# Attention stage: every unit's column sums on TensorE, none of the second pair additions on GpSimd or VectorE

## The chip, the cores and the metric

The kernel runs on one core of a Trainium2 chip. The metric is the device time of one execution in microseconds (us); less is better. The chip's engines run their own instruction streams and meet at semaphores: TensorE (PE, with its weight loads PEld), VectorE (DVE), ScalarE (ACT), GpSimd (POOL), and SyncE (SP), which issues the DMAs.

## What is computed

Eight images of 384 channels and 32 x 32 pixels go through three stages, one after the other on the chip: a convolution with a local correlation, an attention with 12 heads of width 32 over the 1024 pixels, and a feed-forward layer. The change touches the attention alone, of which this is the core (t is the image as 1024 tokens of 384 channels):

```python
q = (x @ Wq.T).reshape(b, n, H, HD).transpose(0, 2, 1, 3)     # H = 12, HD = 32
...
scores = jnp.einsum('bhqd,bhkd->bhqk', q, k) * SCALE
probs = jax.nn.softmax(scores, axis=-1)
out = jnp.einsum('bhqk,bhkd->bhqd', probs, v)
...
t = t + _L1_attn_ref(_ln_t(t), ...)
```

The softmax needs, for each query, the maximum over the keys, the exponentials and their sum. The kernel divides by the sum only after the weighing with v.

## The kernel before, in words

**Units.** The attention works on one image in 24 units (IU): three groups of four heads, eight units in a group. A unit u covers for the four heads two key tiles of 128 (256 keys) and one half of the queries (512 of 1024). So four units (u%4 = 0 to 3) make one block: all keys for one half of the queries, and six blocks x make an image. Scores stand transposed, keys on the partitions and queries along the free axis.

**What a unit does.** TensorE makes 8 score matmuls (`scores`, L892, 4 steps s of 2) into three PSUM banks `st`; ScalarE turns each into exponentials in SBUF (`exponentials`, L1259, tiles `ex`, two sets of four, one per parity of u). TensorE weighs v with the exponentials of the unit before (`weigh(u-1, 0)` and `weigh(u-1, 1)`, L926): each call is four 32-column matmuls of 512 columns in float32, side by side in the array by `tile_position`, and float32 makes two instructions of each, so 8 instructions. They add into the bank `pv`.

**Maxima.** Beside that, 8 matmuls per unit (`max_scores`, L905) make scores of the next group of heads, queries on the partitions, into two banks `mx`, turn by turn; VectorE takes the maximum of each (`take_max`, L1067), which frees its bank. The matmul of item n waits until the reduction of item n-2 is done. Every second unit VectorE folds 16 partial maxima (`combine`, L1073), TensorE transposes them (`turn`, L911), ScalarE copies the row (L1248) and a DMA writes it beside the queries.

**Column sums.** The sum over keys of the exponentials is taken in steps. GpSimd adds the two key tiles of a unit per head (L1416, `pair`, 8 tiles: four per parity). In an odd unit it then adds the pair of the even unit before it (L1420), so that one tile stands for two units. TensorE multiplies it with ones (`sum_up`, L940, again 8 instructions) into the bank `sm`: one such call in every even unit, for the two units before it, and one in the epilogue. In the last eight units of the last image there are no maxima to take, and VectorE makes the second addition (L1145) in GpSimd's place.

**Division.** When a block's sums are complete, VectorE takes their reciprocals in four quarters (`invert_sum`, L1082) and multiplies (`attended`, L1087); ScalarE and GpSimd split the result in high and low halves (L1273, L1352) for the output projection.

**Other work in the units.** In units 6 to 23 the projections of the next image's q, k and v (`project_part`, L854, L864: 5 and 4 matmuls of 512 columns, or 36 of 128), in units 0 to 5 the output projection of the image before (`out_project`, L877). The normalisation of the next image's tokens lies in units 0 to 6, 21 and 23: additions on GpSimd (`fold`, L1366, L1369; also `add`, L1361, in units 0 to 5), VectorE's `centre`, `invert_std`, `normalise`, `z_low` (L1030, L1036, L1042, L1048), and two square roots on ScalarE, each with a change of its function table.

**What sets the order.** Each engine's list is written out by hand in its own `unit(b, u, ...)`; engines are in order. VectorE's list is: `combine` in even units, then for n = 0 to 7 `beside(n)`, which holds the extra work placed at that point, and then the reduction of item n. TensorE's order in a unit is scores 0, projection (5), maximum 0, projection (4), [turn], scores 1, maximum 1, weigh 0, maxima 2 and 3, scores 2, weigh 1, maximum 4, [var or mean], scores 3, maximum 5, [sum_up in even units], maxima 6 and 7. (`maximum(s, e)` is item 2s+e.) A loop covers images 0 to 5; it turns round between units 5 and 6.

Of the kernel before, what the change touches and what calls it, by code (L numbers as in the profile page):

```python
# [17 lines left out]
ALU = mybir.AluOpType  # L18
# [538 lines left out]
def attention_stage(nc, x_in, w_q, w_k, w_v, w_o, b_o, identity, out, n_images):  # L557
# [17 lines left out]
    HG = P // HEAD  # L575
# [16 lines left out]
    with ctx:  # L592
# [74 lines left out]
        pair_added = N.sem("pair_added")  # L667
# [144 lines left out]
        def _(pe):  # L812
# [120 lines left out]
            def sum_up(b, u):  # L933

                w = u % UNITS
                pe.wait_ge(pair_added, STEPS // 2 * (IU * b + u + 1))
                if w % 4 == 1:
                    wait(pe, sum_inverted, 4 * (6 * b + u // 4))
                for h in range(HG):
                    last = nc.tensor.matmul(sm[h * HEAD:(h + 1) * HEAD, :], ones[:, :],  # L940
                                            pair[HG + h][:, :], start=w % 4 == 1,
                                            stop=w % 4 == 3, tile_position=(0, h * HEAD))
                last.then_inc(sum_ready, 1)
# [21 lines left out]
            def unit(b, u, out_proj=True, norm=True, qkv=True, maxima=True, load=False):  # L965
# [3 lines left out]
                lag = (b, u - 1) if u else (b - 1, IU - 1)  # L969
                lagging = not (isinstance(b, int) and b == 0 and u == 0)  # L970
                if u == FIRST and qkv:


                    free[id(pj)] = (std_ready, 2 * b + 4)
# [19 lines left out]
                maximum(0, 1)  # L994
                if lagging:
                    weigh(*lag, 0)
                maximum(1, 0)

                maximum(1, 1)
                scores(b, u, 2)  # L1000
                if lagging:
                    weigh(*lag, 1)
# [8 lines left out]
                if lagging and u % 2 == 0:  # L1011
                    sum_up(*lag)
# [3 lines left out]
            def epilogue(b):  # L1016
                weigh(b, IU - 1, 0)
                weigh(b, IU - 1, 1)
                sum_up(b, IU - 1)
# [6 lines left out]
        def _(dve):  # L1026
# [49 lines left out]
            def invert_sum(b, x, quarter):  # L1076

                at = slice(quarter * QUARTER, (quarter + 1) * QUARTER)
                dve.wait_ge(sum_ready, 2 * (6 * b + x + 1))
# [54 lines left out]
            def unit(b, u, out_proj=True, norm=True, qkv=True, maxima=True, load=False):  # L1134
# [4 lines left out]
                def maximum(s, e):  # L1139
                    if maxima:  # L1140
                        take_max(group, 8 * w + 2 * s + e)
                    elif u % 2 and e == 1:
                        dve.wait_ge(pair_ready, STEPS * (IU * b + u) + s + 1)
                        both = pair[HG + s]
                        nc.vector.tensor_tensor(both[:, :], both[:, :], pair[s][:, :], ALU.add  # L1145
                                                ).then_inc(pair_added, 1)

                def beside(n):

                    if not maxima:  # L1150
                        if u % 4 == 1 and n == 0:
                            for quarter in range(4):
                                invert_sum(b, (u - 5) // 4, quarter)
                            attended(b, (u - 5) // 4)
                        return
                    if started and u % 4 == 1 and n in (0, 1, 7):
                        invert_sum(b, (u - 5) // 4, min(n, 2))
                    if started and u % 4 == 2 and n == 0:
                        invert_sum(b, (u - 6) // 4, 3)
                        attended(b, (u - 6) // 4)  # L1160
# [185 lines left out]
        def _(pool):  # L1346
# [49 lines left out]
            def unit(b, u, out_proj=True, norm=True, maxima=True, load=False, **_flags):  # L1396
                unit_no = IU * b + u
                started = not (isinstance(b, int) and b == 0 and u < 4)
                for s in range(STEPS):
# [9 lines left out]
                    if u % 2 and s == 0:  # L1409

                        wait(pool, sum_ready, IU // 2 * b + u // 2)
                    if u % 2 == 0 and not (isinstance(b, int) and b == 0 and u == 0):

                        pool.wait_ge(pair_added, STEPS // 2 * (unit_no - 2) + s + 1)
# [3 lines left out]
                    if u % 2 and maxima:  # L1418
                        pool.wait_ge(pair_ready, STEPS * unit_no + s + 1)
                        nc.gpsimd.tensor_tensor(both[:, :], both[:, :], pair[s][:, :], ALU.add  # L1420
                                                ).then_inc(pair_added, 1)
# [387 lines left out]
```

## Time and profile before

| what | us |
|---|---|
| median of 3 runs | 3200.16 |
| lowest and highest of the runs | 3199.73, 3200.5 |
| span of the profiled execution, first to last instruction | 3196.4 |
| attention units, first score matmul to the end of the stage | 529.6 to 2371.9 |
| mean granted TensorE clock over the span | 0.948 |

The profiled execution has no time of its own beside its span; the runs are 3.8 us above the span, which is what lies around the instructions. The profile names an engine's instructions by line, with the tiles written and read, and gives for each group the busy time, the mean of one, and the idle time of the engine before it with the one that ended it. The times of a timeline are counted from the first instruction. The duration of a matmul holds the way through the array; the distance from the start of one to the start of the next is what it costs in a stream.

### The profile page before, as it was taken

The numbers are of one execution on the slowest core, as the hardware profiler recorded it, in microseconds if no ns is written. First come the engines' busy times: TensorE is split into PE (matmuls) and PEld (weight loads), VectorE is DVE, ScalarE is ACT, GpSimd is POOL, SyncE is SP. The second block draws the span as 40 slices with busy tenths as digits, with TensorE's granted clock in tenths as the row PEclk, the third lists the DMA queues.
The fourth block names the chain that finished last, engine by engine and source line by source line (L and its number), as shares of the span: only waits on it lengthen the run. The fifth ranks groups of instructions, "written<-read, shape, count | busy, mean of one in ns | idle before, by whom it ended". The sixth has DMA issues, their size and how long they took to land. (4 is left out here: it accounts for less than half of the span.)

```text
span 3196.4 us, 52214 instructions
## 1 busy us (share of the span) xinstructions
PE 2839.4 (89%) x16784; PEld 1108.5 (35%) x16784; DVE 2046.0 (64%) x2855; ACT 1550.0 (48%) x2582; POOL 1851.1 (58%) x1407
## 2 busy tenths in 40 slices
PE   4988668898899898898898898999858999999999
PEld 3544222233233233333332332332113444444444
DVE  6777247878778778778778778777634334334332
ACT  2333023556556556556556556555534444444443
POOL 2222023899899899799899899989951110110110
PEclk9888777999999999999999999999978999999999
DMA  3233222011111111111211211112020011010110
GB/s 140 79 114 104 95 77 66 21 54 27 61 54 28 61 54 28 65 51 28 71 44 28 76 39 34 60 27 67 1 99 20 20 40 35 24 39 20 39 39 20
DMA packets 68759, 163.91 MB, mean 51 GB/s; under 512 B 13585, under 2 KB 17614, under 8 KB 67470
## 3 DMA queue, kind: packets, MB, share of 16 engines
q1 hardware_dynamic: 68494, 160.67, 15.7%
q8 instruction: 131, 2.15, 0.3%
q14 instruction: 134, 1.10, 0.1%
HBM read 59.20 MB, written 37.75 MB: 30 GB/s over the span
## 5 line engine op out<-in xcount | busy, mean ns | idle before, releaser
L1067 DVE TENSOR_REDUCE b_mxp<-b_mx 128x1 f32<-128x512 f32 x1536 | 1002.4, 680 | 375.3 <-PE b_mx L905 368.2
L1416 POOL TENSOR_TENSOR b_pair<-b_ex 128x512 f32<-128x512 f32 x768 | 1001.5, 1313 | 162.9 <-ACT b_ex L1259 152.5
L1259 ACT ACTIVATE b_ex<-b_st 128x512 f32<-128x512 f32 x1536 | 829.2, 595 | 544.1 <-PE b_st L892 540.0
L905 PE MATMUL b_mx<-b_kst,b_qst 96*128 96x512 f16 x1536 | 568.1, 394 | 109.6 <-DVE b_mxp L1067 92.0
L892 PE MATMUL b_st<-b_qst,b_kst 97*128 97x512 f16 x1536 | 472.2, 386 | 32.0 <-issue 17.8
L1420 POOL TENSOR_TENSOR b_pair<-b_pair 128x512 f32<-128x512 f32 x368 | 476.5, 1295 | 28.9
L1630 DVE TENSOR_TENSOR c_gs<-c_g,c_gs 128x512 f16<-128x512 f32 x192 | 132.6, 691 | 466.2 <-ACT c_gs L1703 466.2
L1555 PE MATMUL c_hid<-c_z,c_wi 128*128 128x512 f16 x1728 | 406.8, 381 | 16.4 <-DVE c_z L1623 16.4
L926 PE MATMUL b_pv<-b_ex,b_v 128*32 128x512 f32 x3072 | 412.9, 610 | 1.0 <-ACT b_ex L1259 1.0
L1570 PE MATMUL c_acc<-c_gs,c_wo 128*128 128x512 f16 x1728 | 403.9, 379 | 0.0
L905 PEld LDWEIGHTS b_mx<-b_kst,b_qst 96*128 96x128 f16 x1536 | 132.9, 97 | 716.5 <-DVE b_mxp L1067 597.3
L1736 POOL TENSOR_TENSOR c_xs<-c_x 128x512 f32<-128x512 f32 x16 | 21.1, 1319 | 484.2 <-DMA c_x<-after_attention 481.9
L1699 ACT ACTIVATE c_g<-c_hid,c_bias 128x512 f32<-128x512 f32 x192 | 131.4, 685 | 345.6 <-PE c_hid L1555 345.4
L1555 PEld LDWEIGHTS c_hid<-c_z,c_wi 128*128 128x128 f16 x1728 | 168.4, 98 | 237.5 <-issue 29.6
L1570 PEld LDWEIGHTS c_acc<-c_gs,c_wo 128*128 128x128 f16 x1728 | 169.1, 98 | 203.9
L892 PEld LDWEIGHTS b_st<-b_qst,b_kst 97*128 97x128 f16 x1536 | 149.6, 99 | 190.8 <-ACT b_ex L1259 46.1
L1082 DVE RECIPROCAL b_inv<-b_sm 128x128 f32<-128x128 f32 x192 | 180.4, 944 | 9.3 <-PE b_sm L940 9.3
L506 POOL TENSOR_TENSOR a_sqs<-a_sq 128x1024 f32<-128x1024 f32 x8 | 18.8, 2354 | 218.1 <-ACT a_sq L484 218.1
L854 PE MATMUL b_pj<-b_z,b_wq 128*128 128x512 f16 x405 | 117.2, 420 | 20.6 <-issue 10.8
L1703 ACT ACTIVATE c_gs<-c_g 128x512 f16<-128x512 f32 x192 | 120.9, 629 | 6.1
L1736 POOL TENSOR_TENSOR c_xs<-c_sq 128x512 f32<-128x512 f32 x16 | 20.3, 1266 | 174.0 <-ACT c_sq L1680 174.0
L877 PE MATMUL b_pj<-b_ao,b_wo 128*128 128x512 f16 x432 | 112.3, 409 | 8.5 <-ACT b_ot L1280 6.6
(153 smaller groups left out, 2928.6 us busy)
## 6 DMA issues: line engine op xcount, KB each, us to landing
a_x<-in_x SPq DMA_DIRECT2D x8, 1536.0 KB, 7.1
a_ob<-a_x SPq DMA_DIRECT2D x8, 1536.0 KB, 7.1
after_conv<-a_ob SPq DMA_DIRECT2D x24, 512.0 KB, 2.6
b_xl<-after_conv SPq DMA_DIRECT2D x8, 1536.0 KB, 6.4
b_qst<-b_staged0q SPq DMA_DIRECT2D x192, 64.0 KB, 2.0
b_kst<-b_staged0k SPq DMA_DIRECT2D x192, 64.0 KB, 2.0
b_v<-b_vstaged SPq DMA_DIRECT2D x24, 512.0 KB, 3.0
b_xr<-after_conv SPq DMA_DIRECT2D x8, 1536.0 KB, 6.4
```

What stands on the lines that cost most here:

```text
L892: nc.tensor.matmul(st[(SCORES * u + n) % NST][:, :], kst[g][0:MAXROW + 1, s, kt * P:(kt + 1) * P], qst[g][0:MAXROW + 1, s, half * BANK:(ha ...
L905: nc.tensor.matmul(mx[item % 2][:, :], qst[g][0:MAXROW, h, t * P:(t + 1) * P], kst[g][0:MAXROW, h, half * BANK:(half + 1) * BANK], start=T ...
L926: last = nc.tensor.matmul(pv[h * HEAD:(h + 1) * HEAD, :], v[g][:, kt, h * HEAD:(h + 1) * HEAD], ex[u % 2 * HG + h][:, e * BANK:(e + 1) * B ...
L1067: nc.vector.reduce_max(mxp[h % 2][:, t, half:half + 1], mx[item % 2][:, :], AX_X).then_inc(mx_taken, 1)
L1082: nc.vector.reciprocal(inv[:, at], sm[:, at]).then_inc(sum_inverted, 1)
L1259: nc.scalar.activation(ex[u % 2 * HG + s][:, e * BANK:(e + 1) * BANK], st[(SCORES * u + n) % NST][:, :], ACT.Exp, scale=SCALE).then_inc(ex ...
L1416: nc.gpsimd.tensor_tensor(both[:, :], e[:, 0:BANK], e[:, BANK:NPIX], ALU.add).then_inc(pair_ready, 1)
L1420: nc.gpsimd.tensor_tensor(both[:, :], both[:, :], pair[s][:, :], ALU.add).then_inc(pair_added, 1)
L1555: last = nc.tensor.matmul(hid[m % NH][:, :], wi[a][:, k, m * P:(m + 1) * P], z[p][b][:, k, :], start=n == 0, stop=n == 8)
L1570: last = nc.tensor.matmul(acc[j][:, :], wo[a][:, m, j * P:(j + 1) * P], gs[m % NS][b][:, :], start=m == 0 and n == 0, stop=m == MC - 1 and ...
L1630: nc.vector.tensor_tensor(gs[m % NS][1][:, :], g[m % NG][:, :], gs[m % NS][0][:, :], ALU.subtract).then_inc(glo_ready, 1)
L1699: nc.scalar.activation(g[m % NG][:, :], hid[m % NH][:, :], ACT.Gelu, bias=bias[:, m:m + 1], scale=1.0 / WSCALE).then_inc(gelu_ready, 1)
```

## The change

The second additions (L1420 on GpSimd, L1145 on VectorE) and their semaphore go. `sum_up` is called for every unit, two units late, and takes that unit's own pair tiles. It stands directly before the two calls of `weigh`, which now follow each other, so that TensorE makes 24 float32 instructions in one run. Items 2 and 3 of the maxima and scores 2 are moved around that run. GpSimd waits before the first pair of a unit for the sum of two units before. VectorE's four reciprocals of a block, which stood at n = 0, 1, 7 of the unit u%4 = 1 and n = 0 of the next, all stand at n = 4 to 7 of the unit u%4 = 1.

```diff
--- before.py
+++ after.py
@@ -664,7 +664,6 @@
         st_ready = N.sem("st_ready")
         exp_ready = N.sem("exp_ready")
         pair_ready = N.sem("pair_ready")
-        pair_added = N.sem("pair_added")
         pv_ready = N.sem("pv_ready")
         sum_ready = N.sem("sum_ready")
         pv_moved = N.sem("pv_moved")
@@ -933,12 +932,12 @@
             def sum_up(b, u):
 
                 w = u % UNITS
-                pe.wait_ge(pair_added, STEPS // 2 * (IU * b + u + 1))
-                if w % 4 == 1:
+                pe.wait_ge(pair_ready, STEPS * (IU * b + u + 1))
+                if w % 4 == 0:
                     wait(pe, sum_inverted, 4 * (6 * b + u // 4))
                 for h in range(HG):
                     last = nc.tensor.matmul(sm[h * HEAD:(h + 1) * HEAD, :], ones[:, :],
-                                            pair[HG + h][:, :], start=w % 4 == 1,
+                                            pair[u % 2 * HG + h][:, :], start=w % 4 == 0,
                                             stop=w % 4 == 3, tile_position=(0, h * HEAD))
                 last.then_inc(sum_ready, 1)
 
@@ -967,7 +966,9 @@
                 group = GROUPS * b + g + 1
                 image = b + 1 if g == GROUPS - 1 else b
                 lag = (b, u - 1) if u else (b - 1, IU - 1)
+                before = (b, u - 2) if u > 1 else (b - 1, IU + u - 2)
                 lagging = not (isinstance(b, int) and b == 0 and u == 0)
+                summing = not (isinstance(b, int) and b == 0 and u < 2)
                 if u == FIRST and qkv:
 
 
@@ -992,14 +993,14 @@
 
                 scores(b, u, 1)
                 maximum(0, 1)
+                maximum(1, 0)
+                if summing:
+                    sum_up(*before)
                 if lagging:
                     weigh(*lag, 0)
-                maximum(1, 0)
-
+                    weigh(*lag, 1)
+                scores(b, u, 2)
                 maximum(1, 1)
-                scores(b, u, 2)
-                if lagging:
-                    weigh(*lag, 1)
                 maximum(2, 0)
                 if norm and u in (1, 2):
                     var(b + 1, u - 1)
@@ -1008,14 +1009,13 @@
 
                 scores(b, u, 3)
                 maximum(2, 1)
-                if lagging and u % 2 == 0:
-                    sum_up(*lag)
                 maximum(3, 0)
                 maximum(3, 1)
 
             def epilogue(b):
                 weigh(b, IU - 1, 0)
                 weigh(b, IU - 1, 1)
+                sum_up(b, IU - 2)
                 sum_up(b, IU - 1)
                 for i in range(6):
                     out_project(b, i)
@@ -1076,7 +1076,7 @@
             def invert_sum(b, x, quarter):
 
                 at = slice(quarter * QUARTER, (quarter + 1) * QUARTER)
-                dve.wait_ge(sum_ready, 2 * (6 * b + x + 1))
+                dve.wait_ge(sum_ready, 4 * (6 * b + x + 1))
                 if quarter == 0:
                     wait(dve, att_ready, 6 * b + x)
                 nc.vector.reciprocal(inv[:, at], sm[:, at]).then_inc(sum_inverted, 1)
@@ -1139,25 +1139,15 @@
                 def maximum(s, e):
                     if maxima:
                         take_max(group, 8 * w + 2 * s + e)
-                    elif u % 2 and e == 1:
-                        dve.wait_ge(pair_ready, STEPS * (IU * b + u) + s + 1)
-                        both = pair[HG + s]
-                        nc.vector.tensor_tensor(both[:, :], both[:, :], pair[s][:, :], ALU.add
-                                                ).then_inc(pair_added, 1)
 
                 def beside(n):
 
+                    if started and u % 4 == 1 and n in (4, 5, 6, 7):
+                        invert_sum(b, (u - 5) // 4, n - 4)
+                    if started and u % 4 == 2 and n == 0:
+                        attended(b, (u - 6) // 4)
                     if not maxima:
-                        if u % 4 == 1 and n == 0:
-                            for quarter in range(4):
-                                invert_sum(b, (u - 5) // 4, quarter)
-                            attended(b, (u - 5) // 4)
                         return
-                    if started and u % 4 == 1 and n in (0, 1, 7):
-                        invert_sum(b, (u - 5) // 4, min(n, 2))
-                    if started and u % 4 == 2 and n == 0:
-                        invert_sum(b, (u - 6) // 4, 3)
-                        attended(b, (u - 6) // 4)
                     if n == 3 and u >= FIRST and qkv:
                         stage_low(b + 1, u - FIRST)
                     if load and u in (21, 23) and n in (5, 6):
@@ -1406,19 +1396,11 @@
                     if u < FIRST and out_proj and s == 2:
                         add(b - 1, u)
                     pool.wait_ge(exp_ready, SCORES * unit_no + 2 * s + 2)
-                    if u % 2 and s == 0:
-
-                        wait(pool, sum_ready, IU // 2 * b + u // 2)
-                    if u % 2 == 0 and not (isinstance(b, int) and b == 0 and u == 0):
-
-                        pool.wait_ge(pair_added, STEPS // 2 * (unit_no - 2) + s + 1)
+                    if s == 0 and not (isinstance(b, int) and b == 0 and u < 2):
+                        pool.wait_ge(sum_ready, unit_no - 1)
                     e, both = ex[u % 2 * HG + s], pair[u % 2 * HG + s]
                     nc.gpsimd.tensor_tensor(both[:, :], e[:, 0:BANK], e[:, BANK:NPIX], ALU.add
                                             ).then_inc(pair_ready, 1)
-                    if u % 2 and maxima:
-                        pool.wait_ge(pair_ready, STEPS * unit_no + s + 1)
-                        nc.gpsimd.tensor_tensor(both[:, :], both[:, :], pair[s][:, :], ALU.add
-                                                ).then_inc(pair_added, 1)
 
             def epilogue(b):
                 attended_low(b, 5)
```

## Rows read from the trace of the kernel before

**Rows 1.** Head of the profile's page.
```profile
span 3196.4 us, 52214 instructions
```
**Rows 2.** Busy time by stretch: all units; fourth image, units 0-6 and 7-23.
```profile
core 0: us, PE busy (x) PEld busy (x) DVE busy (x) ACT busy (x) POOL busy (x), PEclk, DMA share, GB/s
529.61:2371.86 1842.25, 1671.32 (x9694) 555.13 (x9692) 1411.94 (x2084) 1068.58 (x1969) 1645.92 (x1284) 0.97 0.14 43
1222.62:1306.20 83.58, 68.21 (x328) 20.92 (x328) 66.33 (x94) 48.83 (x81) 70.54 (x55) 0.92 0.20 65
1306.20:1459.05 152.85, 146.59 (x937) 53.00 (x935) 116.70 (x180) 87.56 (x169) 138.74 (x111) 1.00 0.14 39
```
**Rows 3.** Groups of instructions by line (busy us, mean ns, idle before, by whom ended).
```profile
L1259 ACT ACTIVATE b_ex<-b_st 128x512 f32<-128x512 f32 x1536 | 829.2, 595 | 544.1 <-PE b_st L892 540.0 <-POOL b_pair L1416 2.8
L1420 POOL TENSOR_TENSOR b_pair<-b_pair 128x512 f32<-128x512 f32 x368 | 476.5, 1295 | 28.9
```
**Rows 4.** TensorE's timeline, unit 9 of the fourth image (start us, length us, ...).
```profile
1324.18 1.24 PE L854 MATMUL b_pj<-b_z,b_wk 128*128 128x512 f16 x5
1325.26 0.38 PE L905 MATMUL b_mx<-b_kst,b_qst 96*128 96x512 f16 x1
...
1326.78 0.38 PE L905 MATMUL b_mx<-b_kst,b_qst 96*128 96x512 f16 x1
1327.09 1.06 PE L926 MATMUL b_pv<-b_ex,b_v 128*32 128x512 f32 x8
1328.09 0.60 PE L905 MATMUL b_mx<-b_kst,b_qst 96*128 96x512 f16 x2
...
1331.88 0.39 PE L905 MATMUL b_mx<-b_kst,b_qst 96*128 96x512 f16 x1 [0.26 <-DVE b_mxp L1067]
1332.11 0.60 PE L892 MATMUL b_st<-b_qst,b_kst 97*128 97x512 f16 x2
```
**Rows 5.** TensorE's timeline in the epilogue: two calls of weigh without a break.
```profile
2343.87 1.92 PE L926 MATMUL b_pv<-b_ex,b_v 128*32 128x512 f32 x16 [1.04 <-ACT b_ex L1259]
```
**Rows 6.** VectorE's timeline, end of unit 9 and start of unit 10, same image.
```profile
1328.52 0.69 DVE L1067 TENSOR_REDUCE b_mxp<-b_mx 128x1 f32<-128x512 f32 x1 [0.63 <-PE b_mx L905]
...
1331.13 0.69 DVE L1067 TENSOR_REDUCE b_mxp<-b_mx 128x1 f32<-128x512 f32 x1
...
1332.34 0.95 DVE L1082 RECIPROCAL b_inv<-b_sm 128x128 f32<-128x128 f32 x1
1333.20 0.63 DVE L1067 TENSOR_REDUCE b_mxp<-b_mx 128x1 f32<-128x512 f32 x1
```
**Rows 7.** Busy time by stretch: units 8, 9 and 10 of the fourth image.
```profile
1314.56:1323.75 9.19, 9.08 (x52) 2.88 (x51) 5.76 (x11) 5.50 (x11) 7.83 (x7) 1.00 0.01 2
1323.75:1332.11 8.36, 7.96 (x43) 2.58 (x41) 7.65 (x12) 4.83 (x9) 7.21 (x7) 1.00 0.00 0
1332.11:1341.72 9.61, 9.30 (x79) 3.96 (x77) 7.79 (x13) 5.50 (x11) 9.36 (x8) 1.00 0.01 3
```
**Rows 8.** Duration in ns, least/median/most, of two VectorE lines with two SBUF inputs.
```profile
L1087 DVE TENSOR_TENSOR b_pvs<-b_pvs,b_inv x48: 691/1254/1819, 588.5 to 2351.2; 128x512 f32<-128x512 f32 x48
...
L1042 DVE TENSOR_TENSOR b_xl<-b_xl,b_xs x48: 674/1148/1802, 417.5 to 1983.7; 128x512 f32<-128x512 f32 x48
```
**Rows 9.** Busy time by stretch: last image, units 0-5, 6-15 and 16-22.
```profile
2156.74:2209.73 52.99, 51.31 (x274) 15.76 (x273) 37.33 (x59) 31.71 (x60) 51.27 (x42) 1.00 0.15 41
2209.73:2289.88 80.15, 69.51 (x366) 16.98 (x365) 62.53 (x99) 46.55 (x90) 78.66 (x63) 0.98 0.11 40
2289.88:2337.23 47.35, 37.49 (x202) 7.14 (x201) 29.67 (x25) 31.36 (x61) 46.66 (x35) 0.92 0.00 1
```
**Rows 10.** GpSimd's timeline in those last units.
```profile
2310.92 6.17 POOL L1416 TENSOR_TENSOR b_pair<-b_ex 128x512 f32<-128x512 f32 x5
```
**Rows 11.** Busy time by stretch: two neighbouring stretches inside units 3 and 4, fourth image.
```profile
1261.69:1265.10 3.41, 1.24 (x5) 0.19 (x2) 3.41 (x5) 2.14 (x3) 3.33 (x3) 1.00 0.00 0
1265.10:1268.52 3.42, 3.25 (x8) 1.25 (x9) 3.13 (x6) 1.51 (x3) 3.34 (x4) 0.50 0.00 0
```

## The prediction

> **What bounds the kernel now.** I read the busy times by stretch first, then the waits, then the timelines of one unit. The attention is 1842 of the 3196.4 us of the span [rows 1, 2], and the change touches nothing outside it. In it GpSimd is busy 1646 us, TensorE 1671, VectorE 1412: the first looks like a bound. It is not: ScalarE, which must wait for the pair tiles, lost only 2.8 us to them over all units [rows 3]. The 368 second additions, 476.5 us of GpSimd [rows 3], are hidden work.
>
> TensorE sets the pace in units 7 to 23: 146.6 of 152.9 us busy [rows 2]. At the end of unit 9 it waits for VectorE, which must free a bank of the maxima [rows 4], while VectorE has idle time in the same unit (7.65 of 8.36 us busy [rows 7]). So the order of the two lists counts, not the load alone. In units 0 to 6 the stretch is 83.6 us: VectorE 66.3 busy, GpSimd 70.5, TensorE 68.2 [rows 2]. There the normalisation is on VectorE, and some 6 us of unit 6 are a stall at the loop's turn, which the change leaves.
>
> **TensorE's own work.** Float16 matmuls of 512 columns start 0.22 us apart (five in 1.08 us), a float32 call starts 0.31 after the matmul before it, and the next float16 matmul 1.00 after its start [rows 4]. Two calls without a break take 1.92 us against 1.06, so each further call costs 0.86 [rows 5]. Before, two units held five calls, 5 x (1.00 + 0.09) = 5.45 us. After, each holds a run of 2.72 (1.00 + 2 x 0.86) plus 0.09, 5.62 for two. The extra sums cost TensorE only 0.09 us per unit, some 16 us over 192 units.
>
> **The new wait: a plain unit.** The run is 2.7 us in which no bank of the maxima is written, so VectorE has only items 1 and 2 (and what stands at n = 1 to 3) to do and then idles. Behind it stand five maxima, 3 to 7, with four score matmuls. Take the first matmul behind the run as 0. Scores 2 are at 0.00 and 0.22, maxima 3 and 4 at 0.44 and 0.66, scores 3 at 0.88 and 1.10. A reduction starts 0.43 after its matmul (1328.09 to 1328.52), the next ones follow at about 0.6 to 0.65, and the matmul that needs the bank starts 0.75 after the start of the reduction that frees it (1331.13 to 1331.88) [rows 4, 6]. So reductions 3 and 4 start at 0.87 and 1.50, maxima 5, 6, 7 at 1.62, 2.25, 2.87, and the next unit's scores at 3.10, where without waits it would be 1.96. Then scores, five projection matmuls, maximum 0 at 4.62, four more, scores 1, maxima 1 and 2 at 6.14 and 6.36; the run starts at 6.67 and ends at 9.39. **A plain step is 9.4 us**, against 8.36 in unit 9 [rows 7]. Where the next unit has a turn and VectorE does not hold it anyway, the turn and the wait for its row come on top. Unit 8, with a turn and one call more, took 9.19; unit 9 without its idle 0.40 and with 1.09 for a call is 9.05, and without all of its waits (three of the maxima, some 0.8) 8.65 [rows 7]. So the turn is between 0.14 and 0.54; I take 0.37, nearer to the second, since overlapping durations hide idle time: 9.75.
>
> **The reciprocals.** They stand at n = 4 to 7, behind maximum 3, which stands behind the run: VectorE cannot reach them in its idle time, though the sums are ready by then. Each adds 0.86 (1332.34 to 1333.20 [rows 6]). From reduction 3 at 0.87: reciprocal 1.48, reduction 4 at 2.34, 5 at 3.81, 6 at 5.28, 7 at 6.75, combine 7.4, `attended` 7.5. This takes 0.69 alone and 1.25 in the median [rows 8]. GpSimd will have ended its four pairs at about 3.9 and waits for the next run, so I take 0.69. Reduction 0 starts at 8.1, maximum 2 at 8.9, the run at 9.2. **The step from u%4 = 1 is 11.9 us**, chained on VectorE. Before, units 9 and 10 together took 17.97 [rows 7]; these two steps take 21.3.
>
> **Units 7 to 23 of an image.** Eight plain steps 75.0, four with a turn 39.0, three of 11.9 make 35.7, the step from unit 21 with three centrings (0.6 each) 13.7, that from 23 with three 10.3: 173.7 against 152.9 [rows 2], so +21 per image, **+146 us** over seven images.
>
> **Units 0 to 6.** The same chain, with 0.6 to 0.9 for each piece of the normalisation at n = 4 to 7 and at n = 0 of the next unit, gives 9.4, 11.9 (from unit 1), 11.6 (my estimate, where ScalarE's square root holds the next exponentials), 10.4, 10.0, 12.7 (from unit 5), 10.0 and the 6 us stall: 82 against 83.6 [rows 2]. VectorE's 66.3 us of work are there on either side, so I take **0**, with -3 to +5 per image as bounds.
>
> **Last image.** Units 0 to 5: three plain, one with a turn, two of 11.9 give 61.7 against 53.0. Units 6 to 15 have no projection; a plain step is then 7.7 and two of ten are 11.9: 86.3 against 80.2 [rows 9]. **+15.** Units 16 to 22 took 47.35 [rows 9], held by the additions on GpSimd and VectorE; without the second ones GpSimd's five pairs in 6.17 us [rows 10] make 4.9 per unit, 34.5 in all. Some of it will be handed over to waits: **-10**, bounds -14 and 0. The epilogue gets one more sum and loses one addition: 0.
>
> **The clock.** In a stretch of 3.41 us TensorE was busy for 1.24 us, waiting for VectorE at full clock; in the next 3.42 us the granted clock was 0.50 (1.2 GHz) [rows 11]. In the step from u%4 = 1 three matmuls stand in some 3.4 us, which looks alike. It is followed by projections with 0.8 us to spare before VectorE is the later one again; at half clock eight matmuls lose 1.7. I estimate 0.35 per such step on the mean, 47 times: **+16**. Bounds: nothing, and 1.7 each, +80.
>
> **New waits that I cost at nothing.** GpSimd's first pair waits for the sum of u-2, some 1.6 us before the run's end; its four pairs (1.23 each [rows 10]) then end at about 3.9 of a step of 9.4, and ScalarE needs them a unit later. Behind this wait stand GpSimd's folds and `add`; they have the freed 476 us as cover. If that cover failed, ScalarE's wait for pairs would grow from 2.8 us. The staging of the projection (n = 3) falls in VectorE's idle time. SP's queue is not touched.
>
> **Sum.** 146 + 0 + 15 - 10 + 16 = 167 us. On the span, 3196.4 + 167 = 3363; on the median of the runs, which is 3.8 above the span, **3367 us**.
>
> **A rule against the trace.** Multiplications on VectorE took from 674 and 691 to over 1800 ns [rows 8], so something shares with them. This gives a rival: with GpSimd quiet, all 96 instructions of these two lines fall to about 0.68, which is 48 x 0.57 + 48 x 0.47 = 50 us less on VectorE. The Trainium skill ("SBUF — State Buffer", Who interferes with whom) states that a VectorE instruction with two SBUF inputs contends with a GpSimd instruction that reads SBUF, the one that issues first holding the port for its whole length. The trace agrees, with the spread above; by that rule GpSimd's fewer additions speak for the change.
>
> **Rivals.**
> - *Faster, about 3156 us* (chance 0.05). The place is units 0 to 6 of each image, where VectorE and GpSimd are both over 79% busy [rows 2]. If the 50 us come off there, VectorE uses the run to get ahead, and the last units give 10, it is 3200 - 50 - 10 + 16 for the sums. It decides where the step from u%4 = 1 stays under 9.1 us. Against it: four reciprocals alone are 3.4 us behind the run.
> - *No change, about 3205* (0.03). Only TensorE's work counts, +16 and -10, because the maxima's waits stay as they are. Against it: the wait is there now, with three maxima in a row [rows 4].
> - *Plain steps only, about 3270* (0.08). VectorE is faster over the reciprocals than I chain them: 10 us per image are left of the 21 (each of four such steps at 9.4), 70 in seven images.
> - *The clock, about 3440* (0.12). Half clock follows each of the 47 long steps and also catches the float32 run, 1.7 us each.
> - *My forecast, 3367* (0.72).
>
> The range, 3290 to 3440, takes in the bounds of the units 0 to 6, of the last units and most of the clock. A measurement of this kernel tells 0.2% from no change; faster 0.05, same 0.03, slower 0.92.
>
> **What would show it.** In the profile after: a run of 24 float32 instructions of about 2.8 us in each unit; 12 units of 9.4 and 9.75 among units 7 to 23, and 11.9 where the reciprocals are; three waits of TensorE for VectorE before maxima 5, 6 and 7, some 1.1 us in a plain unit; GpSimd's busy time down by about 476 us; `attended` near 0.69 us; reciprocals beginning only behind maximum 3. I am wrong if the plain step is under 9 us, if VectorE takes reciprocals during the run, or if the clock of units 7 to 23, now 1.00 [rows 2], falls below 0.9.

## The result, and the profile after

The changed kernel takes 3434.5 us (median of 4 runs, 3425.3 to 3435.3) against 3200.3: a ratio of 1.073, 95% interval 1.0715 to 1.0745. The forecast was 3367, range 3290 to 3440. The profiled execution took 3425.3 us; its span is 3422.8, 226 above that of before [rows 1]. It was the fastest of the four, 9 us under the median, so the parts below are compared with the forecast of the span, 3363.

The page of the changed kernel (busy us, mean ns, idle before and who ended it):

```profile
span 3422.8 us, 52829 instructions
...
PE 2960.8 (87%) x17552; PEld 1200.9 (35%) x17552; DVE 1962.8 (57%) x2839; ACT 1531.3 (45%) x2582; POOL 1358.1 (40%) x1039
...
L1402 POOL TENSOR_TENSOR b_pair<-b_ex 128x512 f32<-128x512 f32 x768 | 974.5, 1287 | 935.3 <-PE b_sm L939 814.7
L1249 ACT ACTIVATE b_ex<-b_st 128x512 f32<-128x512 f32 x1536 | 810.7, 598 | 801.9 <-PE b_st L891 799.4
L904 PE MATMUL b_mx<-b_kst,b_qst 96*128 96x512 f16 x1536 | 554.8, 399 | 219.7 <-DVE b_mxp L1067 193.5
```

Two rows of the full list of groups, ScalarE's exponentials now and TensorE's maxima before:

```profile
L1249 ACT ACTIVATE b_ex<-b_st 128x512 f32<-128x512 f32 x1536 | 810.7, 598 | 801.9 <-PE b_st L891 799.4 <-POOL b_pair L1402 1.9
L905 PE MATMUL b_mx<-b_kst,b_qst 96*128 96x512 f16 x1536 | 568.1, 394 | 109.6 <-DVE b_mxp L1067 92.0 <-ACT b_ex L1259 1.3 <-ACT b_mr L1248 0.3
```

GpSimd's second additions are gone and it waits 815 us for the sums, as the code asks. This new wait holds up nobody: ScalarE's idle time is again ended by TensorE, and it waited 1.9 us for pair tiles where it was 2.8 [rows 3]. TensorE is the one that waits longer: 194 us for VectorE before the maxima, where it was 92.

By stretch, same columns as [rows 2]: fourth image, units 0-6 and 7-23, units 8, 9, 10 and 14 of it, and the last image's units 0-5, 6-15 and 16-22:

```profile
1314.39:1401.32 86.93, 69.82 (x352) 23.27 (x352) 63.56 (x94) 48.24 (x81) 51.86 (x40) 0.92 0.19 62
1401.32:1578.21 176.89, 159.15 (x1008) 61.99 (x1007) 111.65 (x180) 85.94 (x169) 94.46 (x78) 0.96 0.12 34
1412.01:1421.69 9.68, 9.02 (x51) 3.17 (x51) 5.83 (x11) 5.39 (x11) 4.99 (x5) 1.00 0.01 2
1421.69:1432.61 10.92, 8.75 (x50) 3.02 (x49) 7.28 (x12) 4.73 (x9) 6.03 (x5) 1.00 0.00 0
1432.61:1442.78 10.17, 9.43 (x79) 4.24 (x78) 7.38 (x13) 5.45 (x11) 4.51 (x4) 1.00 0.01 2
1472.83:1483.96 11.13, 10.49 (x52) 3.48 (x50) 7.95 (x14) 5.37 (x11) 4.50 (x4) 0.87 0.13 52
2360.40:2424.11 63.71, 57.19 (x298) 18.69 (x297) 36.21 (x59) 31.03 (x60) 39.20 (x32) 0.95 0.15 44
2424.11:2518.22 94.11, 79.84 (x407) 21.13 (x405) 60.60 (x99) 45.30 (x90) 52.09 (x44) 0.89 0.07 28
2518.22:2567.32 49.10, 42.67 (x227) 10.44 (x225) 10.20 (x13) 29.70 (x60) 36.24 (x29) 0.90 0.00 1
```

Units 7 to 23 took 152.85 us before [rows 2] and 176.89 now. The last image grew from 52.99, 80.15 and 47.35 [rows 9] to 63.71, 94.11 and 49.10. TensorE's timeline in unit 9, from the run on, and the start of VectorE's behind it:

```profile
1425.25 1.06 PE L939 MATMUL b_sm<-b_pair,b_ones 128*32 128x512 f32 x8
1426.13 1.90 PE L925 MATMUL b_pv<-b_ex,b_v 128*32 128x512 f32 x16
1427.96 0.60 PE L891 MATMUL b_st<-b_qst,b_kst 97*128 97x512 f16 x2
1428.40 0.60 PE L904 MATMUL b_mx<-b_kst,b_qst 96*128 96x512 f16 x2
1428.84 0.60 PE L891 MATMUL b_st<-b_qst,b_kst 97*128 97x512 f16 x2
1429.57 0.39 PE L904 MATMUL b_mx<-b_kst,b_qst 96*128 96x512 f16 x1
1430.98 0.39 PE L904 MATMUL b_mx<-b_kst,b_qst 96*128 96x512 f16 x1 [1.02 <-DVE b_mxp L1067]
1432.38 0.39 PE L904 MATMUL b_mx<-b_kst,b_qst 96*128 96x512 f16 x1 [1.01 <-DVE b_mxp L1067]
1432.61 0.60 PE L891 MATMUL b_st<-b_qst,b_kst 97*128 97x512 f16 x2
```

```profile
1428.83 0.69 DVE L1067 TENSOR_REDUCE b_mxp<-b_mx 128x1 f32<-128x512 f32 x1 [1.79 <-PE b_mx L904]
1429.43 0.95 DVE L1082 RECIPROCAL b_inv<-b_sm 128x128 f32<-128x128 f32 x1
1430.30 0.63 DVE L1067 TENSOR_REDUCE b_mxp<-b_mx 128x1 f32<-128x512 f32 x1
```

This is the chain that was forecast: the run lasts 2.71 us, and VectorE sits idle for 1.79 us until maximum 3. Then it takes a reciprocal between each two reductions, and each of the matmuls of maxima 6 and 7 waits a full microsecond for it.

### The profile page after: what moved, and what is told of

Same layout as the page of the kernel before. It is cut to its first block and busy times, and to the rows that moved or that the text cites. A ratio compares the mean times of both kernels' runs of the same rounds, so it can differ in the third digit from the quotient of the medians.

```text
span 3422.8 us, 52829 instructions
## 1 busy us (share of the span) xinstructions
PE 2960.8 (87%) x17552; PEld 1200.9 (35%) x17552; DVE 1962.8 (57%) x2839; ACT 1531.3 (45%) x2582; POOL 1358.1 (40%) x1039
## 5 line engine op out<-in xcount | busy, mean ns | idle before, releaser
L1067 DVE TENSOR_REDUCE b_mxp<-b_mx 128x1 f32<-128x512 f32 x1536 | 982.7, 678 | 667.9 <-PE b_mx L904 665.4
L1402 POOL TENSOR_TENSOR b_pair<-b_ex 128x512 f32<-128x512 f32 x768 | 974.5, 1287 | 935.3 <-PE b_sm L939 814.7
L1249 ACT ACTIVATE b_ex<-b_st 128x512 f32<-128x512 f32 x1536 | 810.7, 598 | 801.9 <-PE b_st L891 799.4
L891 PE MATMUL b_st<-b_qst,b_kst 97*128 97x512 f16 x1536 | 488.8, 394 | 40.3 <-ACT b_ex L1249 19.7
L925 PE MATMUL b_pv<-b_ex,b_v 128*32 128x512 f32 x3072 | 373.0, 604 | 1.1 <-ACT b_ex L1249 1.1
L904 PEld LDWEIGHTS b_mx<-b_kst,b_qst 96*128 96x128 f16 x1536 | 150.2, 98 | 553.6 <-DVE b_mxp L1067 420.9
L939 PE MATMUL b_sm<-b_pair,b_ones 128*32 128x512 f32 x1536 | 212.2, 626 | 0.0
L925 PEld LDWEIGHTS b_pv<-b_ex,b_v 128*32 128x32 f32 x3072 | 101.9, 113 | 242.4 <-issue 200.6
L863 PE MATMUL b_pj<-b_wv,b_z 128*128 128x128 f16 x1620 | 122.6, 239 | 7.0 <-DVE b_xl L1030 7.0
L863 PEld LDWEIGHTS b_pj<-b_wv,b_z 128*128 128x128 f16 x1620 | 114.5, 109 | 26.7 <-DVE b_xl L1030 10.0
```

The lines of the kernel that those rows point to most:

```text
L863: last = nc.tensor.matmul(bank[:, t * P:(t + 1) * P], z[a][:, k, at:at + P], ws[2][b][:, k, g * P:(g + 1) * P], start=n == 0, stop=n == 8)
L891: nc.tensor.matmul(st[(SCORES * u + n) % NST][:, :], kst[g][0:MAXROW + 1, s, kt * P:(kt + 1) * P], qst[g][0:MAXROW + 1, s, half * BANK:(ha ...
L904: nc.tensor.matmul(mx[item % 2][:, :], qst[g][0:MAXROW, h, t * P:(t + 1) * P], kst[g][0:MAXROW, h, half * BANK:(half + 1) * BANK], start=T ...
L925: last = nc.tensor.matmul(pv[h * HEAD:(h + 1) * HEAD, :], v[g][:, kt, h * HEAD:(h + 1) * HEAD], ex[u % 2 * HG + h][:, e * BANK:(e + 1) * B ...
L1067: nc.vector.reduce_max(mxp[h % 2][:, t, half:half + 1], mx[item % 2][:, :], AX_X).then_inc(mx_taken, 1)
L1249: nc.scalar.activation(ex[u % 2 * HG + s][:, e * BANK:(e + 1) * BANK], st[(SCORES * u + n) % NST][:, :], ACT.Exp, scale=SCALE).then_inc(ex ...
```

## The experiments

Where a text below speaks of time at half clock, it is the sum, over the attention's units, of the stretches that the trace records with a granted clock of 0.50: 104 us before, 247 us in the changed kernel. Where a text below gives sums over several images, they are counted from 0 (the fourth image is image 3). Unless the text says otherwise, sums over units 0 to 6 are of images 1 to 6, and those over units 7 to 23 of images 0 to 6. Ratios are to the kernel before, which was run beside each experiment and took 3196.1 to 3201.5 us there. The second experiment's kernel is called the split version.

**No second additions.** From before, L1420 and L1145 with their semaphore are removed, and `sum_up` waits for `pair_ready`. The kernel leaves the even units out of the sums. One of the places:

```diff
-                    if u % 2 and maxima:
-                        pool.wait_ge(pair_ready, STEPS * unit_no + s + 1)
-                        nc.gpsimd.tensor_tensor(both[:, :], both[:, :], pair[s][:, :], ALU.add
-                                                ).then_inc(pair_added, 1)
```

> The kernel before without any second pair addition (none on GpSimd, none on VectorE): the column sums take the odd units alone, so the sums of the even units are left out of the result. TensorE's and the other lists are those of before. My theory (the additions were hidden work, TensorE and its waits for VectorE set the pace): 3185 to 3200 us, where the last eight units give up to 10 us and quieter multiplications on VectorE a few more. Rival (GpSimd's load was a bound, or its port sharing with VectorE cost time on the path): 3150 us or less.

Measured: 3178.6 us, ratio 0.993 (0.992 to 0.995). Units 7 to 23 of the fourth image, and units 16 to 22 of the last:

```profile
1302.41:1454.48 152.07, 146.18 (x936) 53.01 (x935) 115.62 (x180) 87.61 (x169) 95.03 (x77) 1.00 0.14 39
...
2280.73:2318.21 37.48, 34.27 (x203) 6.96 (x201) 11.65 (x13) 31.26 (x61) 36.08 (x29) 1.00 0.01 1
```

GpSimd's busy time falls from 138.7 to 95.0 us in units 7 to 23 of this image, and they take 152.1 us instead of 152.9 [rows 2]. The additions were nearly hidden there: over seven images these units gain 8 us. Of the 23 us that the span is shorter, 10 are the last units, 47.35 [rows 9] to 37.48. The time is 6 us under the range that I expected, but far from the rival's (GpSimd as a bound, 3150 or less), which falls. Units 0 to 6 of images 0 to 6, where GpSimd's relief might have helped VectorE most, took 565 us against 560.

**The change's sums in the order of before.** From the changed kernel:

```diff
-                maximum(1, 0)
-                if summing:
-                    sum_up(*before)
                 if lagging:
                     weigh(*lag, 0)
-                    weigh(*lag, 1)
-                scores(b, u, 2)
+                maximum(1, 0)
                 maximum(1, 1)
+                scores(b, u, 2)
+                if lagging:
+                    weigh(*lag, 1)
...
                 maximum(2, 1)
+                if lagging:
+                    sum_up(*lag)
                 maximum(3, 0)
...
-                sum_up(b, IU - 2)
                 sum_up(b, IU - 1)
...
-                    if started and u % 4 == 1 and n in (4, 5, 6, 7):
-                        invert_sum(b, (u - 5) // 4, n - 4)
+                    if started and u % 4 == 1 and n in (0, 1, 2, 4):
+                        invert_sum(b, (u - 5) // 4, min(n, 3))
```

> The change's sums (each unit's own pair tiles, no second additions) in the order of before: weigh 0, weigh 1 and sum_up stand apart, sum_up before maximum 6 of every unit, reciprocals at n = 0, 1, 2, 4. My theory (the loss is made by the run of 24 and by where the reciprocals stand, not by the sums): only odd units grow, by 0.3 to 1.1 us each, so 3230 to 3305 us, 3270 as the likeliest; units 7 to 23 of an image about 160 us. Rival (TensorE's extra sums are the loss): 3400 us or more.

Measured: 3169.9 us, ratio 0.990 (0.989 to 0.992). This is 60 us under the range of my theory (3230 to 3305) and far from the rival's. Fourth image, units 0-6 and 7-23, then units 9, 10 and 11, and the last units; below them TensorE in unit 11:

```profile
1216.55:1294.37 77.82, 67.93 (x353) 20.67 (x352) 63.10 (x93) 48.67 (x81) 53.39 (x41) 0.98 0.21 69
1294.37:1448.83 154.46, 152.85 (x1008) 53.72 (x1007) 114.91 (x181) 87.44 (x169) 96.23 (x77) 1.00 0.14 39
1312.18:1321.28 9.10, 8.79 (x50) 2.74 (x49) 8.76 (x14) 4.83 (x9) 5.44 (x5) 1.00 0.00 0
1321.28:1330.43 9.15, 9.05 (x78) 3.90 (x77) 6.01 (x11) 5.47 (x11) 6.29 (x6) 1.00 0.01 2
1330.43:1339.22 8.79, 8.79 (x78) 3.80 (x76) 5.31 (x9) 4.83 (x9) 5.07 (x5) 1.00 0.01 2
2273.26:2312.78 39.52, 36.54 (x227) 7.21 (x225) 10.58 (x13) 31.69 (x61) 36.59 (x30) 1.00 0.01 2
```

```profile
1337.03 0.60 PE L891 MATMUL b_st<-b_qst,b_kst 97*128 97x512 f16 x2
1337.47 0.38 PE L904 MATMUL b_mx<-b_kst,b_qst 96*128 96x512 f16 x1
1337.78 1.07 PE L939 MATMUL b_sm<-b_pair,b_ones 128*32 128x512 f32 x8
1338.78 0.60 PE L904 MATMUL b_mx<-b_kst,b_qst 96*128 96x512 f16 x2
```

The call costs 1.09 us, but it stands where TensorE waited for VectorE, between maxima 5 and 6, and no wait is left in unit 11: 8.79 us, all of it busy, against 8.43 before. Unit 9, which has the four reciprocals as well, goes from 8.36 [rows 7] to 9.10, and unit 10 falls from 9.61 [rows 7] to 9.15. Over the whole kernel TensorE's wait for VectorE before the maxima falls from 92 to 43 us. With the extra sums units 7 to 23 grow by only 12 us over seven images, so the loss is not theirs.

**The split version again, on another chip.**

> The kernel of e2 a second time, in more rounds: 3165 to 3175 us, a ratio to before of 0.987 to 0.993 with an upper end below 0.998, if its gain over before holds on another chip.

Measured: 3171.8 us, ratio 0.992 (0.990 to 0.993). This version beats both kernels, the one before by 0.8 to 1.0%.

**The reciprocals in VectorE's idle time.** From the changed kernel, whose run stays:

```diff
-                    if started and u % 4 == 1 and n in (4, 5, 6, 7):
-                        invert_sum(b, (u - 5) // 4, n - 4)
-                    if started and u % 4 == 2 and n == 0:
+                    if started and u % 4 == 1 and n == 3:
+                        invert_sum(b, (u - 5) // 4, 0)
+                        invert_sum(b, (u - 5) // 4, 1)
+                    if started and u % 4 == 2 and n < 2:
+                        invert_sum(b, (u - 6) // 4, n + 2)
+                    if started and u % 4 == 2 and n == 2:
                         attended(b, (u - 6) // 4)
...
+                exponentials(b, u, 1)
                 if started and u % 4 == 2:
                     attended_high(b, (u - 6) // 4)
-                exponentials(b, u, 1)
```

> The changed kernel with the run as it is, but the four reciprocals where VectorE idles: two at n = 3 of the unit u%4 = 1, two at n = 0 and 1 of the next, the multiplication at n = 2, and ScalarE's copy of its result one step later. My theory: the unit pair u%4 = 1, 2 goes from some 22.1 us to 19.0 to 19.5, half clock in the attention from 247 us to 120 to 160, in all 3260 to 3310 us. Rival (the plain steps and the extra sums make nearly all of the loss): 3390 us or more.

Measured: 3334.9 us, ratio 1.041 (1.040 to 1.043). Units 0-6, 7-23, 9 and 10 of the fourth image:

```profile
1281.98:1369.20 87.22, 67.38 (x352) 22.72 (x352) 64.09 (x94) 48.47 (x81) 53.42 (x41) 0.94 0.19 62
1369.20:1534.13 164.93, 154.39 (x1008) 59.72 (x1007) 112.02 (x180) 86.52 (x169) 93.39 (x77) 0.99 0.13 36
1389.89:1399.20 9.31, 8.76 (x51) 3.02 (x49) 7.33 (x12) 4.73 (x9) 4.98 (x5) 1.00 0.00 0
1399.20:1408.93 9.73, 9.08 (x78) 4.25 (x77) 7.41 (x13) 5.53 (x11) 5.54 (x5) 1.00 0.01 2
```

The pair of units is 19.04 us, as expected. The place of the reciprocals, with the clock that it costs, was worth 100 us. I had expected 125 to 175, so this time was missed: units 0 to 6 gave nothing back (87.2 us against 86.9; half clock 145 us, most of it now in units 5 to 7). Against the split version, which has the same sums, 165 us are left. They lie as much in units 0 to 6 as behind them: over images 0 to 6, units 0 to 6 take 605 us against 532, and units 7 to 23 take 1153 against 1079.

**Filler matmuls.** In the changed kernel, maxima 5 and 6 of units u%4 = 1 are made four times:

```diff
+                for _ in range(more + 1):
+                    made = nc.tensor.matmul(mx[item % 2][:, :], ...)
+                made.then_inc(mx_ready, 1)
...
+                                   more=3 if u % 4 == 1 and 2 * s + e in (5, 6) else 0)
```

> The changed kernel with maxima 5 and 6 of each unit u%4 = 1 made four times over (same inputs, same bank, the last one counts), in time in which TensorE waits for VectorE anyway. The clock theory: TensorE is no longer idle there, half clock in the attention falls from 247 us to 110 to 150 and the unit behind (u%4 = 2) from 10.1 to 12.3 us to a steady 10.2; 3370 to 3405 us. Rival (the spread of those units is not the clock's): 3425 to 3440 us, or slower by the extra matmuls.

Measured: 3387.2 us, ratio 1.058 (1.056 to 1.059); half clock 142 us. Units 9 and 10:

```profile
1408.48:1419.40 10.92, 10.04 (x57) 3.45 (x55) 7.27 (x12) 4.73 (x9) 6.02 (x5) 1.00 0.01 2
1419.40:1429.57 10.17, 9.43 (x79) 4.24 (x78) 7.38 (x13) 5.45 (x11) 4.51 (x4) 1.00 0.00 0
```

Six more matmuls in unit 9 leave its 10.92 us as they were, and the kernel with more work is 47 us faster: 105 us less at half clock. Where the unit behind had 11.13 us at a granted 0.87 (unit 14 of the changed kernel, above), it now takes 10.05. Half clock in units 7 to 23 of images 0 to 6 falls from 109 to 13 us, and these units from 1237 to 1206 us.

**The run alone, with the sums of before.** From before: `sum_up` (even units), `weigh` 0 and 1 in the changed kernel's place.

```diff
+                maximum(1, 0)
+                if lagging and u % 2 == 0:
+                    sum_up(*lag)
                 if lagging:
                     weigh(*lag, 0)
-                maximum(1, 0)
-                maximum(1, 1)
+                    weigh(*lag, 1)
                 scores(b, u, 2)
-                if lagging:
-                    weigh(*lag, 1)
+                maximum(1, 1)
...
-                if lagging and u % 2 == 0:
-                    sum_up(*lag)
                 maximum(3, 0)
```

> The kernel before with its second additions and its one sum per two units, but TensorE's order of the changed kernel: sum_up (in even units), weigh 0 and weigh 1 in one run behind maximum 2, and maxima 3 to 7 behind it. My theory (the run costs through the maxima's two banks, whatever the sums are): an odd plain unit 8.5 us where it was 8.4, an even one 9.7 where it was 9.0 to 9.2, half clock in the attention above 104 us; 3240 to 3290 us. Rival (the run is harmless while it holds fewer calls): 3190 to 3210 us.

Measured: 3369.5 us, ratio 1.053 (1.051 to 1.056); half clock 241 us. Units 9 and 10 and the last image's 16 to 22, then two rows of its list of waits (total us, times, longest):

```profile
1395.50:1403.94 8.44, 7.89 (x42) 2.75 (x41) 7.35 (x12) 4.73 (x9) 7.52 (x7) 1.00 0.00 0
1403.94:1414.95 11.01, 9.27 (x79) 4.25 (x78) 8.10 (x13) 5.50 (x11) 9.06 (x8) 1.00 0.01 2
2450.16:2514.45 64.29, 44.76 (x202) 10.08 (x201) 30.22 (x25) 29.62 (x60) 43.94 (x33) 0.79 0.00 1
```

```profile
PE b_sm L940 <- POOL b_pair L1418: 27.1, 12, 3.4
PE b_sm L940 <- DVE b_pair L1143: 11.1, 4, 3.4
```

The plain steps came as forecast, 8.4 and 9.6 to 9.7, but the time is 80 us above the range. The expectation missed three things. Unit 10 is 11.0, because before's last reciprocal at n = 0 and a multiplication now stand in the chain that the run waits for (maximum 2, just before the run, waits 1.09 us for VectorE). The sum's earlier place meets second additions that are not ready: a sum early in a unit waits for GpSimd, and in the last eight units for VectorE, which makes these additions there. The third is units 0 to 6: over images 0 to 6 they go from 560 to 629 us, as much as units 7 to 23 (1067 to 1134), and nearly half of that is unit 2, from 12 or 13 us to 16 or 17 in each image. So the new order loses time without any of the new sums, though here the waits for the second additions are part of the loss.

**A run of two.** The split version with `weigh` 0 and 1 together behind maximum 2, the sum still before maximum 6.

```diff
+                maximum(1, 0)
                 if lagging:
                     weigh(*lag, 0)
-                maximum(1, 0)
-
-                maximum(1, 1)
+                    weigh(*lag, 1)
                 scores(b, u, 2)
-                if lagging:
-                    weigh(*lag, 1)
+                maximum(1, 1)
```

> The kernel of e2 (every unit's own sum before maximum 6), but weigh 0 and weigh 1 in one run behind maximum 2 as in the changed kernel, maximum 3 behind scores 2. My theory (what counts is what stands between the five maxima behind the run): a run of two is 0.86 us shorter than one of three, and the sum behind maximum 5 takes the place of two waits, so a plain unit is 8.8 us where e2 has 8.75; 3160 to 3195 us. Rival (every unbroken run costs, by the idle time it gives VectorE): 3220 us or more.

Measured: 3200.7 us, ratio 1.001 (1.000 to 1.002), a little outside what I expected. Unit 11 of the fourth image:

```profile
1346.90:1355.76 8.86, 8.72 (x78) 3.99 (x77) 5.16 (x9) 4.73 (x9) 5.05 (x5) 1.00 0.01 2
```

8.86 us against 8.79. So with the same sums: no run 3170, a run of two 3201, a run of three with the reciprocals placed well 3335, and placed behind it 3434. (From the second to the third the sum also moves from u-1 to u-2, and the reciprocals' places differ, so the length of the run is not the only thing that changes there.)

**The last units.** In the changed kernel, `weigh` 1 stands behind scores 2 where there are no maxima.

```diff
                 if lagging:
                     weigh(*lag, 0)
+                if lagging and maxima:
                     weigh(*lag, 1)
                 scores(b, u, 2)
+                if lagging and not maxima:
+                    weigh(*lag, 1)
```

> The changed kernel, but in the last eight units of the last image, which have no maxima, weigh 1 stands behind scores 2 instead of in the run. My theory of why those units did not get shorter (during the run no scores are made, there are three banks for them, so ScalarE's exponentials and the run follow one another): units 16 to 22 of the last image take 37 to 44 us where the changed kernel took 49; the rest unchanged, about 3420 to 3430 us. Rival (GpSimd's pairs or its new wait hold them): 48 to 50 us.

Measured: one run, 3423.8 us. The last image's units 16 to 22, and the changed kernel's timeline there:

```profile
2520.84:2562.56 41.72, 36.93 (x226) 8.34 (x225) 10.09 (x13) 30.20 (x59) 35.42 (x29) 1.00 0.01 1
```

```profile
2535.40 1.90 PE L925 MATMUL b_pv<-b_ex,b_v 128*32 128x512 f32 x16
...
2537.23 0.82 PE L891 MATMUL b_st<-b_qst,b_kst 97*128 97x512 f16 x3
2537.74 3.05 ACT L1249 ACTIVATE b_ex<-b_st 128x512 f32<-128x512 f32 x6 [1.62 <-PE b_st L891]
...
2538.39 2.35 PE L891 MATMUL b_st<-b_qst,b_kst 97*128 97x512 f16 x5 [0.34 <-ACT b_ex L1249]
```

49.1 us became 41.7: the unbroken run was what held them. ScalarE stands still until scores come behind the run, three banks are filled at once, and the other five matmuls wait for exponentials. The granted clock of these units rose from 0.90 to 1.00 with it, which may be part of the 7.4 us.

**Where the split version's gain over before comes from.** Before, with that version's places of the reciprocals:

```diff
-                    if started and u % 4 == 1 and n in (0, 1, 7):
-                        invert_sum(b, (u - 5) // 4, min(n, 2))
+                    if started and u % 4 == 1 and n in (0, 1, 2, 4):
+                        invert_sum(b, (u - 5) // 4, min(n, 3))
                     if started and u % 4 == 2 and n == 0:
-                        invert_sum(b, (u - 6) // 4, 3)
```

> The kernel before in every respect (second additions, one sum per two units, its order), but with e2's places of the reciprocals: n = 0, 1, 2, 4 of the unit u%4 = 1, none in the next. It tells apart where e2's gain over before comes from. If it is the places: 3170 to 3185 us, units 0 to 6 of an image some 78 us and half clock in the attention near 36 us, as in e2. If it is the sums on TensorE (a call in TensorE's waits of the odd units, quieter GpSimd): 3192 to 3205 us with half clock near 104 us. I take a share of both: the unit u%4 = 2 goes from 9.6 to 9.2 us, 3185 to 3197 us.

Measured: 3197.0 us, ratio 0.999 (0.998 to 1.000); units 0 to 6 from 491 to 486 us (466 in the split version), half clock 101 us. Unit 10 takes 9.15 us as there, but unit 9 before it 9.02: the places alone give almost nothing. Nor does the relief of GpSimd alone, by the first experiment.

**Filler before.** Before, with maxima 2 to 7 of units 2 to 6 made twice (`more=1 if 2 <= u <= 6 and 2 * s + e >= 2 else 0`), and the same in the split version:

> The kernel before with maxima 2 to 7 of units 2 to 6 made twice over (same inputs, same bank), some 1.3 us of TensorE work per unit where it waits for VectorE. If e2's gain in units 0 to 6 (491 to 466 us over images 1 to 6) is TensorE kept at full clock by the extra calls: half clock in the attention falls from 104 us to under 70 and these units to 470 to 482 us, 3182 to 3194 us in all. Rival (the gain is not the clock's): 3198 to 3210 us.

> e2 with the same doubled maxima in units 2 to 6. e2 has only 36 us of half clock left, most of it at the loop's turn, where a stall of instructions is the cause: little to win, 3165 to 3175 us. If the doubled matmuls stood in VectorE's way it would be 3180 us or more.

Measured: 3200.6 us, ratio 1.001 (1.000 to 1.002), and 3196.4 us, ratio 0.999 (0.998 to 1.000). Before's half clock fell to 53 us, units 0 to 6 from 491 only to 483: what the clock gave, the doubled matmuls took. What they cost by themselves shows in units 0 to 6 of the last image, which are at full clock with and without them: 62.4 us became 68.1. In the split version the filler cost 25 us (3171.8 to 3196.4) and left 40 us of half clock where there were 36, so my expectation of 3165 to 3175 was wrong, and the case that I named beside it, doubled matmuls in VectorE's way, fits the time. Full clock bought with work in these units is worth nothing here. What makes the split version 25 us faster in them stays open.

## Why the prediction was right, and where its sizes were off

The direction, the mechanism and the two chains on VectorE were right. The parts, from the starts of the units in the two traces (images counted from 0):

| part | forecast | measured |
|---|---|---|
| units 7 to 23, seven images | +146, and most of +16 for the clock | 1066.9 to 1237.2: +170 |
| units 0 to 6, images 0 and 1 to 6 | 0 | 69.3 to 78.2 and 490.8 to 516.4: +34 |
| last image, units 0 to 15 | +15 | 133.1 to 157.8: +25 |
| last image, units 16 to 22 | -10 | 47.4 to 49.1: +2 |
| the rest of the span | 0 | -5 |

Of the 59 us by which the span exceeds its forecast, 34 are in units 0 to 6. The range held the time by 5 us.

- **A plain step 9.4, with a turn 9.75.** Units 11 and 8 took 9.4 and 9.68. Right.
- **The reciprocals, 21.3 for the pair.** 10.92 + 10.17 = 21.09 where the clock held. Where it did not, such a pair took more: 22.2 us for units 13 and 14 of the same image. `attended` fell to a median of 691 ns, from 1254 [rows 8], as taken. The other line with two SBUF inputs, `xl`, fell less (a mean of 1192 to 1012 ns), so both together lost 36 us and not the 50 of the faster rival. The Trainium skill's rule of the shared port ("SBUF — State Buffer", Who interferes with whom) agrees with the shorter `attended`, but the gain is 0.55 us in a few steps and decides nothing.
- **TensorE's own work, some 16 us.** The run took 2.71 us, for the 2.72 taken. What the extra sums cost TensorE in this order alone no run shows. In the split version, whose extra calls stand in waits, units 7 to 23 grow by 12 us in seven images against before, and by 16 against before with the same places of the reciprocals (1063 to 1079).
- **The clock was mis-sized.** I priced it at 0.35 us per step on the mean, 16 us; the filler, in 46 such units, gives 47 us back by itself (30 us between the two profiled executions).
- **"Some of it will be handed over to waits: -10"** is the step that failed. I costed the last units by GpSimd's additions and did not ask what the run does to ScalarE through the three banks of scores. Removing the additions alone does give 10 us (first experiment); in the changed kernel these units took 49.1 us, 2 more than before, and 41.7 with the run broken up.
- **Units 0 to 6 at nothing** failed as well: I took it that VectorE's load is the same on either side. It is about the same (66.3 and 63.6 us in the fourth image), and yet these units grew. Over images 0 to 6 they take 560 us before, 532 in the split version, 541 with a run of two, 605 with a run of three and the reciprocals placed well, and 595 in the changed kernel. So with the same sums the new order costs 63 us there, and the 34 are what is left behind the 29 that the split version wins for a reason not found. That the growth stayed within the bound of 5 us per image is luck: neither of the two was forecast. That VectorE's work cannot be done while the run lasts is my explanation; it was not tested alone.
- **Last image, units 0 to 15.** The steps as listed add up to 85.4 us for units 6 to 15, not 86.3, so the term was 14 and not 15; 25 were measured, and the filler gives 5 of them back.
- The rivals: that GpSimd's relief wins was refuted by the first experiment, "plain steps only" by the place of the reciprocals costing 100 us. The clock rival described part of the truth. Its 3440 is closest to the time, but it got there with 1.7 us per step, where the filler gives back 1.0.

## What to carry to other kernels

Grouping matmuls of one kind into one run saves little on TensorE (0.23 us per call here), and no bank of scores or maxima is filled while it lasts: here VectorE stood idle for 1.79 us and ScalarE for 1.62 us. Look at what stands behind the run, for it comes at those engines' pace. Put an added call where TensorE already waits for another engine, and put an engine's side work where that engine's list reaches it during its idle time, not behind the instruction that ends the idle time. An engine that is busy nearly all the time (GpSimd, 89% of the attention; TensorE 91%) can be off the path: taking 476 us of work from it gave 23 us. Read who ended the others' waits.

## What was unexpected about the hardware

TensorE's granted clock fell though none of the waits just before was long. In the changed kernel waits of about 1.0 us between single matmuls, as in unit 9 above, were followed in many images by a granted clock of 0.50 in the next unit (2.6 to 6.0 us of it in unit 10 of five of the first seven images). Six more matmuls in the same waits removed all of that in unit 10 of those images, and took the whole kernel from 3434.5 to 3387.2 us. But doubled matmuls in units 2 to 6 did nothing for the kernel before: half clock fell from 104 to 53 us and the time stayed.
